# An attention and expert kernel on Trainium2: context transposed as fp16 integers, x transposed in fp32

## What is computed

```python
q = (xb * (FP8_MAX / safe)).astype(jnp.float8_e4m3fn)      # safe = maximum(amax, eps)
xq = q.astype(jnp.float32) * (safe / FP8_MAX)              # x: blocks of 1 x 128
wq = ...                                                   # ctx: the same in blocks of 128 x 128
x = x + einsum('emk,enk->emn', quant_dequant(layernorm(x)), quant_dequant(ctx))
x = x + ffn(layernorm(x))
```

## Time and profile before

| | |
|---|---|
| median of 3 runs | 6937.68 us |
| the profiled execution | 6961.73 us, span 6960.1 us |
| busy over the span | PE 93%, POOL 48%, PEld 44%, DVE 26%, ACT 15% |
| mean granted TensorE clock | 0.973 of full speed |
| chain that ended last | PE 84%, DVE 5%, DMA 5%, issue 4% |

### The profile page before, as it was taken

One profiled execution on the slowest core, in us unless ns is written; L12 is line 12 of the kernel. 1 busy time (PEld: TensorE's weight loads), 2 busy tenths in 40 slices (PEclk: granted clock), 3 DMA queues, 4 the chain that ended last, 5 costly groups with the idle time before them and its releaser, 6 DMA issues.

```text
span 6960.1 us, 89515 instructions
## 1 busy us (share of the span) xinstructions
PE 6482.9 (93%) x32742; PEld 3083.2 (44%) x32743; DVE 1808.4 (26%) x2650; ACT 1030.8 (15%) x1206; POOL 3371.1 (48%) x2161
## 2 busy tenths in 40 slices
PE   3666779999999999999999999999999999999998
PEld 1333334444444444444444444444444444444444
DVE  7999850001111111111111111111111111115555
ACT  2444411111111111111111111111111111110000
POOL 5665754336544445544455545554465456442222
PEclk9788889999999999999999999999999999999999
DMA  2333449995555555555555555555566556559887
GB/s 81 115 127 112 151 134 345 277 342 152 152 157 140 140 147 153 153 158 140 144 156 152 157 143 159 150 156 147 141 164 166 140 151 169 150 143 248 258 258 226
DMA packets 1146758, 1175.24 MB, mean 169 GB/s; under 512 B 867296, under 2 KB 867296, under 8 KB 1146720
## 3 DMA queue, kind: packets, MB, share of 16 engines
q10 hardware_dynamic: 902352, 477.20, 29.1%
q1 hardware_dynamic: 184464, 487.80, 21.5%
q0 software_dynamic: 59904, 209.75, 8.6%
HBM read 647.63 MB, written 327.16 MB: 140 GB/s over the span
## 4 chain that ended last, share of the span: by engine, by line
PE 84%; DVE 5%; DMA 5%; issue 4%; ACT 1%; POOL 1%; DVEq 0%; ACTq 0%; SPq 0%; POOLq 0%
PE ps_gu L626 54%; PE ps_d L626 25%; DMA hT<-hid_hl 3%; PE ps_d L761 2%; DMA wts<-in_ctx 2%; PE ps_d L759 2%; DVE wts L1115 1%; ACT wts L865 1%; DVE amax L1068 1%; DVE max_rows L1072 0%; PE ps_t L617 0%; PE ps_gu L617 0%; DVE wts L1159 0%; DVE max_all L1079 0%; DVE to_q L1111 0%
## 5 line engine op out<-in xcount | busy, mean ns | idle before, releaser
L626 PE MATMUL ps_gu<-wts,xT 128*128 128x512 f16 (+1 forms) x19584 | 3927.5, 362 | 9.2 <-DVEq L1357 4.0
L626 PEld LDWEIGHTS ps_gu<-wts,xT 128*128 128x128 f16 x19584 | 1890.1, 98 | 2042.2 <-issue 121.9
L626 PE MATMUL ps_d<-wts,hT 128*128 128x512 f16 x8160 | 1817.4, 381 | 47.5 <-DMA hT<-hid_hl 47.5
L467 POOL TENSOR_SCALAR wts<-stage 128x1408 f16<-128x1408 f32 (+1 forms) x476 | 587.1, 1233 | 2260.1 <-PE ps_d L761 2242.0
L1269 DVE SCALAR_TENSOR_TENSOR hid<-ps_gu,sil 128x704 f32<-128x704 f32 x272 | 242.5, 892 | 4581.1 <-ACT sil L958 4581.1
L470 POOL TENSOR_TENSOR wts<-stage,wts 128x1408 f16<-128x1408 f32 (+1 forms) x476 | 1231.3, 2587 | 39.7
L626 PEld LDWEIGHTS ps_d<-wts,hT 128*128 128x128 f16 x8160 | 798.5, 98 | 1009.1 <-DMA hT<-hid_hl 42.9
L958 ACT ACTIVATE sil<-ps_gu 128x704 f32<-128x704 f32 x272 | 205.9, 757 | 2863.4 <-PE ps_gu L626 2863.4
L468 POOL TENSOR_SCALAR stage<-stage 128x1408 f32<-128x1408 f32 (+1 forms) x476 | 628.2, 1320 | 0.0
L980 ACT ACTIVATE dout<-ps_d 128x1024 f32<-128x1024 f32 x240 | 245.6, 1023 | 2162.8 <-DMA xT<-xin 1940.3
L626 PE MATMUL ps_d<-wts,xin 128*128 128x512 f16 x1536 | 366.1, 398 | 50.7 <-DVE wts L1159 38.7
(11 more groups left out here) (158 smaller groups left out, 2381.3 us busy)
## 6 DMA issues: line engine op xcount, KB each, us to landing
rows_d<-dout ACTq DMA_DIRECT2D x240, 512.0 KB, 3.3
xin<-rows_x ACTq DMA_DIRECT2D x211, 512.0 KB, 3.3
stage<-in_L_ffn_w_down SPq DMA_DIRECT2D x384, 256.0 KB, 3.2
stage<-in_L_ffn_w_gate SPq DMA_DIRECT2D x256, 352.0 KB, 3.2
stage<-in_L_ffn_w_up SPq DMA_DIRECT2D x256, 352.0 KB, 3.7
wts<-in_x SPq DMA_DIRECT2D x64, 512.0 KB, 3.7
rows_x<-wts SPq DMA_DIRECT2D x64, 512.0 KB, 2.9
wts<-rows_x SPq DMA_DIRECT2D x64, 512.0 KB, 6.9
```

The source lines that it names most:

```text
L467: g.tensor_scalar(high, raw, WSCALE, 1.0, ALU.mult, ALU.mult).then_inc(conv_step, 1)
L626: ins = nc.tensor.matmul(dst[c], left, right[c], start=(first and a == 0), stop=(last and a == 2))
```

## The change

**Context.** GpSimd only subtracts rnd and writes the result, a number that fp16 holds exactly, as fp16 into q_ctx (`unround_ctx`). TensorE transposes that alone, eight fp16 transposes. The factor, the same number for all columns of the block, is kept for every tile in from_c and applied after the transposes: ScalarE writes the high half with eight scaled copies of 128 columns from PSUM, and VectorE writes the low half with eight instructions of 128 columns (`ctx_low`), which multiply, subtract the high half and then free ps_t_ctx.

**x.** GpSimd subtracts and multiplies (`dequantise_x`), with a new wait until TensorE has transposed the tile before. TensorE transposes the fp32 result, eight transposes with ident_f; ScalarE writes the high half in one instruction, VectorE the low half (`low_of_q`), which frees ps_t for the next set.

**Maximum.** L1079 becomes a tensor_scalar that reads ps_max (PSUM) and takes the maximum with max_one.

**Orders.** GpSimd takes dequantise_x, unround_ctx, low_of_x2 in a round. In VectorE's round low_of_q(i + 1) stands after ctx_spread, before the moments of x, and ctx_low(i + 8) after the scale of x, before quantise. In the first context rounds ctx_low(c - 1) follows quantise(c); ctx_low(7) follows quantise of x tile 0, and low_of_q(0) follows quantise(1). high_of_nat and low_of_nat are gone. The diff without the lists of semaphores, ScalarE's calls in the first rounds and the removed functions:

```diff
+        from_c = sb("from_c", [P, TT, KH], F32)
-        nat = [pair(area, 4) for area in (early, at_start)]
+        q_ctx = area_rows(at_start, 4)[:, 0:H]
...
-        ps_t_ctx = ps_gu[:, 2:4, :].rearrange("p a n -> p (a n)").bitcast(F16).rearrange("p (a d) -> p a d", a=2)
+        ps_t_ctx = ps_gu[:, 2, :].bitcast(F16).rearrange("p (k n) -> p k n", k=KH)
+        ps_t_x = ps_t[:, :, :].rearrange("p a d -> p (a d)").bitcast(F32).rearrange("p (k n) -> p k n", k=KH)
...
+            def dequantise_x(i):
+
+                pool.wait_ge(rounded[X], i + 1)
+                g.tensor_tensor(quant[X], quant[X], rnd[X], ALU.subtract).then_inc(unrounded_x, 1)
+                pool.wait_ge(unrounded_x, i + 1)
+                if not isinstance(i, int) or i > 0:
+                    pool.wait_ge(tr_done, set_of_x(i - 1) + 1)
+                g.tensor_tensor(deq[X].rearrange("p (k n) -> p k n", k=KH),
+                                quant[X].rearrange("p (k n) -> p k n", k=KH),
+                                from_q[:, X, :].unsqueeze(2).to_broadcast([P, KH, P]),
+                                ALU.mult).then_inc(deq_ready[X], 1)
+
+            def unround_ctx(c):
+
+                pool.wait_ge(rounded[CTX], c + 1)
+                pool.wait_ge(ctr_done, c + 1)
+                pool.sem_inc(pool_turn, 1)
+                g.tensor_tensor(q_ctx, quant[CTX], rnd[CTX], ALU.subtract).then_inc(deq_ready[CTX], 1)
...
-                dequantise(X, i + (LEAD - 1))
+                dequantise_x(i + (LEAD - 1))
                 if ctx:
-                    dequantise(CTX, i + (CLEAD - 1))
-                low_of_nat(X, i + (LEAD - 1))
-                if ctx:
-                    low_of_nat(CTX, i + (CLEAD - 1))
+                    unround_ctx(i + (CLEAD - 1))
...
-                pe.wait_ge(nat_ready[CTX], c + 1)
+                pe.wait_ge(deq_ready[CTX], c + 2)
                 pe.wait_ge(ctr_free, c + 1)
-                transposes(nat[CTX], ps_t_ctx).then_inc(ctr_done, 1)
+                for k in range(KH):
+                    last = nc.tensor.transpose(ps_t_ctx[:, k, :], q_ctx[:, k * P:(k + 1) * P], ident[:, :])
+                last.then_inc(ctr_done, 1)
...
-                tr(nat[X], set_of_x(i), nat_ready[X], i + 1)
+                pe.wait_ge(deq_ready[X], i + 2)
+                pe.wait_ge(tr_free, set_of_x(i) + 1)
+                for k in range(KH):
+                    last = nc.tensor.transpose(ps_t_x[:, k, :], deq[X][:, k * P:(k + 1) * P], ident_f[:, :])
+                last.then_inc(tr_done, 1)
...
-                take(cT[b % 2][:, 0, :, ds(j * P, P)], cT[b % 2][:, 1, :, ds(j * P, P)], ps_t_ctx).then_inc(ctr_free, 1)
+                act.sem_inc(act_turn, 1)
+                for k in range(KH):
+                    last = a.activation(cT[b % 2][:, 0, k, ds(j * P, P)], ps_t_ctx[:, k, :], ACT.Copy, scale=scale_of_ctx(c, k))
+                last.then_inc(ctx_high, 1)
 
             def take_q(i):
                 act.wait_ge(tr_done, set_of_x(i) + 1)
-                take(xqT[:, 0], xqT[:, 1], ps_t).then_inc(tr_free, 1)
+                a.activation(xqT[:, 0], ps_t_x, ACT.Copy).then_inc(q_high, 1)
...
-                v.tensor_copy(max_all[:, :], max_one[:, :].to_broadcast([P, P])).then_inc(max_spread, 1)
+                v.tensor_scalar(max_all[:, :], ps_max[:, 0, :], max_one[:, :], None, ALU.max).then_inc(max_spread, 1)
+
+            def ctx_low(c, j, b):
+                dve.wait_ge(ctx_high, c + 1)
+                dve.sem_inc(dve_turn, 1)
+                for k in range(KH):
+                    last = v.scalar_tensor_tensor(out=cT[b % 2][:, 1, k, ds(j * P, P)], in0=ps_t_ctx[:, k, :],
+                                                  scalar=scale_of_ctx(c, k), in1=cT[b % 2][:, 0, k, ds(j * P, P)],
+                                                  op0=ALU.mult, op1=ALU.subtract)
+                last.then_inc(ctr_free, 1)
+
+            def low_of_q(i):
+                dve.wait_ge(q_high, i + 1)
+                v.tensor_tensor(xqT[:, 1], ps_t_x, xqT[:, 0], ALU.subtract).then_inc(tr_free, 1)
...
-                    v.tensor_scalar(from_q[:, kind, :], safe[:, kind, :], 1.0 / FP8_MAX, scale, ALU.mult, ALU.mult)
+                    factor = from_q[:, X, :] if kind == X else from_c[:, ds(n, 1), :].rearrange("p a k -> p (a k)")
+                    v.tensor_scalar(factor, safe[:, kind, :], 1.0 / FP8_MAX, scale, ALU.mult, ALU.mult)
...
-            def beside(i, x=True, ctx=True, before=True):
+            def beside(i, x=True, ctx=True, before=True, low=None):
 
                 if ctx:
                     ctx_max(i + CLEAD)
                 residual(i)
                 if ctx:
                     ctx_spread(i + CLEAD)
+                if not isinstance(i, int) or i < TT - 1:
+                    low_of_q(i + 1)
                 if x:
                     x_moments(i + LEAD)
                 x2_scale(i)
                 if x:
                     x_scale(i + LEAD)
+                if low is not None:
+                    ctx_low(i + BT, *low)
...
+            ctx_max(0)
+            ctx_spread(0)
+            quantise(c=0)
+            with dve.Fori(1, BT) as c:
                 ctx_max(c)
                 ctx_spread(c)
                 quantise(c=c)
+                ctx_low(c - 1, c - 1, 0)
             x_moments(0)
             x_scale(0)
             quantise(0)
+            ctx_low(BT - 1, BT - 1, 0)
...
+                if i == 1:
+                    low_of_q(0)
+            beside(0, before=False, low=(0, 1))
+            beside(1, before=False, low=(1, 1))
+            with dve.Fori(2, BT) as i:
+                beside(i, low=(i, 1))
+            with dve.Fori(BT, 2 * BT) as i:
+                beside(i, low=(i - BT, 2))
+            with dve.Fori(2 * BT, TT - CLEAD) as i:
+                beside(i, low=(i - 2 * BT, 3))
```

75 lines of the change are left out of this document (23 added, 52 removed).

## The result

| | before | after |
|---|---|---|
| median | 6940.47 us (20 runs, 6922.35 to 6995.44) | 6882.59 us (20 runs, 6862.61 to 6977.27) |
| profiled execution, span | 6960.1 us | 6889.9 us |
| mean granted TensorE clock | 0.973 | 0.975 |

The ratio is 0.9915, with a 95% interval of 0.99 to 0.9931: the change makes the kernel 58 us faster. The forecast was 6880. The total agrees far better than the terms behind it do, as the stages and then the experiments show.

A forecast was written before the change was run, and what follows sets the result against it. It took the attention stage to be bound by VectorE, standing still while GpSimd holds their shared ports. Terms -34 - 5 - 13 - 11 + 5 = -58 us, from 6937.7 to a 6880 median, range 6845 to 6915.

The forecast's parts named there:

- L1079 -1.06: Tiles with context: the spread of the maximum, reading PSUM, falls from 1.38 to 0.32 us, saving 1.06 us a tile.
- L1111 -3.8: Tiles with context: both GpSimd subtractions L485 go, so two VectorE waits at to_q vanish, 3.8 us a tile.
- L1115 and the one collision, -1.9 + 2.0: Tiles with context: L1115's wait on GpSimd's L490 goes (-1.9 us), but L490 still holds up one VectorE instruction (+2.0).
- ctx_low +2.1: Tiles with context: eight VectorE instructions of 128 elements from PSUM add 2.1 us a tile, bounds 1.6 to 2.8.
- L1167's wait +0.25: Tiles with context: ScalarE's eight scaled copies make VectorE's L1167 wait 0.25 us longer for std_l.
- normalise_q covered, -0.5: Tiles with context: ctx_low fills the 0.5 us that VectorE's L1068 waited for ScalarE's normalise_q.
- First context tiles and up to the first product, -13 forecast: Before the attention tiles: removed waits outweigh added low-half work, rounds giving -12.5 us and the rest -0.8, together -13.
- Tiles without context, -11 forecast: Seven periods fall from 19.61 to 18.05 us each, bound by residual, low_of_q and product; together -11 us.
- The last two products, +5 forecast: End of the attention stage, bound by TensorE: products start 1.7 and 3.0 us later behind low_of_q, +5 us.
- slices that are dearer: Rival: each ctx_low instruction costs 0.48 instead of 0.26 us, giving back 39 us, total 6919; chance 0.2.
- L490 misses VectorE: Rival: GpSimd's L490 falls beside reductions or behind L1129 in context tiles too, 22 x 2.0 us more gained, 6836; chance 0.1.
- The slow product: Rival: attention products stay at the lower TensorE clock after idle gaps, +104 us, 7042; chance 0.06 with all else slower.

The follow-up runs named there:

- the last version: The changed kernel with context taken as x is, low_of_x2 moved into the next round's dequantise_x, and low_of_q and ctx_low(31) earlier; 6789.98 us, ratio 0.9784.

## Why the prediction was right, and where it wasn't

The mechanism was right: GpSimd's instructions hold VectorE, L1111 fell to its own time, and two spare instructions bring the cost back. The total was right to 3 us by luck, since misses of both signs cancelled.

**Tiles with context, -1.7 forecast, -2.36 measured.** Term by term:
- L1079 -1.06: it took 0.351 and not 0.32, so the duration holds. Its worth doesn't: 0.26 alone, 0.41 on top of x, 0.18 when undone. The step that failed is to count it on the path without asking what VectorE waits for next.
- L1111 -3.8: held (2 x (2.08 - 0.31) = 3.5).
- L1115 and the one collision, -1.9 + 2.0: the meeting costs 1.65, of which 0.77 falls on top_w; leaving it out gave 1.4.
- low_of_q +1.13 and its wait +0.1: 1.215, no wait. The fp32 transposes take 1.92 us for eight at the lower clock, 0.24 each (0.26 forecast).
- ctx_low +2.1: 2.17, and 0.28 of issue before it, which I left out.
- L1167's wait +0.25: wrong in sign. The waits for std_l (0.36) are gone. I compared ScalarE's eight copies (2.18 us) with the two passes they replace, but not x's one pass with the two before, in the same queue: 0.9 us less ahead of the square root.
- normalise_q covered, -0.5: held.
- "VectorE's wait for the context load stays as it is": it fell from 0.75 to 0.32.

These make -2.5 of the -2.36.

**First context tiles and up to the first product, -13 forecast, -9.0 measured.** A round is 10.3 us instead of the 9.8 of the sum (11.7 - 1.9), a gain of 1.4 and not 1.9; 0.35 of the difference is ctx_low's 2.45 us for the 2.1. The run with context taken as x shows what the slices cost in this stretch, 6.8 us.

**Tiles without context, -11 forecast, -5.9 measured.** The five periods 24 to 28 sum to 89.4, forecast 5 x 18.05 = 90.3, set by residual, low_of_q and product as said. The step that failed is "(7 periods)": rounds 22 and 23 have no context for `quantise`, but still a ctx_low on VectorE. With x alone they take 18.6 and 17.7 us, with the change 21.2 and 23.0, the second because `attend` waits for the last ctx_low at a change of batch. 2.6 + 5.3 = 8 us, the same 8 by which all seven differ (133.6 against 125.6). `attend` names that wait in its first lines, `pe.wait_ge(ctr_free, (b + 1) * BT + 1)`. I had looked at what ctx_low costs VectorE, not at who waits for it.

**The last two products, +5 forecast, +7.4 measured.** The starts of the products are as forecast, 4.4 us behind the residual. The missed term is the clock: the last product before followed an idle time of 1.4 us and got its first 18 matmuls into 4.06 us at a granted clock of 1.00, the one after follows 3.1 us of idle time and needs 5.75, at 0.69. The product ahead of it was slow before too, at 0.69, and is slower after, at 0.57: another 1.2 us. The timelines, the last product before and after:

```profile
880.89 4.06 PE L626 MATMUL ps_d<-wts,xin 128*128 128x512 f16 x18 [1.44 <-ACT xin L836]
885.68 6.64 PE L626 MATMUL ps_d<-wts,xin 128*128 128x512 f16 x30
```

```profile
817.76 5.75 PE L633 MATMUL ps_d<-wts,xin 128*128 128x512 f16 x18 [3.07 <-DVE xin L1089]
824.23 6.64 PE L633 MATMUL ps_d<-wts,xin 128*128 128x512 f16 x30
```

The rivals: slices that are dearer didn't come in the form I gave them (0.27 us apart, not 0.48), though slices did cost 1.0 a tile against doing without. "L490 misses VectorE" didn't come by itself, but moving the instruction gave 41 us, nearly that rival's 44. The slow product came in part. Of products 3 to 22 two were slow in their first 18 matmuls before (over 5 us instead of 4.06), and ten are after, though each reaches the full clock behind them. It costs nothing in tiles with context, where these products still end 4 to 5 us ahead of the residual, except at the two changes of batch; so the limit of that rival, a product of more than 21 us, wasn't reached, and the mean granted clock there is 0.82 (0.81 before). At the last two products it did cost, as said.

What stays open: the 8.5 us behind residual 31 of the profiled execution, and why the gains by medians differ from those at residual 31 by up to 12 us either way (151 and 144 for the last version, 63 and 55 for x alone, 59 and 71 for x with the maximum). It also isn't shown what makes the wait for the context load come and go (0.75 us a tile before, 0.3 after, none with x alone). One profiled execution per kernel can't tell.

## What to carry to other kernels

Price a removed wait only after asking what the engine would wait for next. With VectorE, ScalarE, a load and TensorE within a microsecond of each other, one term of this change was worth a quarter of its duration, and one part alone gave as much as all of it. Where two engines hold each other up, first look for a stretch in which the busy one doesn't mind: one GpSimd instruction moved into it was worth two thirds of a rewrite. And when a step moves to another engine, list who waits for its end, at the loop's edges too, since the tiles at a change of batch behave unlike those between.
